# Scores ahead of value products in every beat of a cross attention, and another end of that stage

## The reference, cut to what matters

```python
q = (layernorm(x) @ wq.T + bq)            # 16 heads of 32
k = ctx @ wk.T + bk; v = ctx @ wv.T + bv  # 8 x 2048 x 512, the same width
attn = softmax(q @ k.T / sqrt(32), axis=-1)
x = x + (attn @ v) @ wo.T + bo            # y: the output projection
x = x + differential_attention(layernorm(x)); x = x + experts(layernorm(x))
```

## Time and profile before

| | us |
|---|---|
| median of 3 runs | 1677.9 |
| lowest, highest | 1677.11, 1684.54 |
| the profiled execution's own time | 1679.28 |
| its span, first to last instruction | 1677.5 |
| TensorE busy | 1608.8 (96%) |
| VectorE, ScalarE, GpSimd busy | 1166.9, 954.1, 932.3 |
| mean granted TensorE clock | 0.979 |

### The profile page before, as it was taken

How to read it: one execution, slowest core, us unless ns; L and a number is a source line. 1 busy time by engine, 2 the same in 40 slices (tenths; PEclk the granted TensorE clock), 3 DMA queues, 4 the chain that set the end, 5 groups by cost and what they waited for, 6 DMA issues and landing times. The chain is left out here.

```text
span 1677.5 us, 36990 instructions
## 1 busy us (share of the span) xinstructions
PE 1608.8 (96%) x15556; PEld 1302.3 (78%) x15556; DVE 1166.9 (70%) x1506; ACT 954.1 (57%) x1445; POOL 932.3 (56%) x498
## 2 busy tenths in 40 slices
PE   7999999999999999999999999677998899999999
PEld 6788888888888888888888888566886677777787
DVE  6137888888888888888888887756434677653322
ACT  4347677777677776777776776753102777630000
POOL 1227788788888878888887885322000344522220
PEclk9999999999999999999999999778999999899999
DMA  8422222222222222222222211203432111211001
GB/s 179 96 40 39 35 42 36 36 38 40 39 38 38 36 36 41 40 36 38 38 39 37 42 23 61 74 3 108 163 88 88 58 45 52 66 51 50 29 22 51
DMA packets 333876, 88.61 MB, mean 53 GB/s; under 512 B 284656, under 2 KB 317168, under 8 KB 333712
## 3 DMA queue, kind: packets, MB, share of 16 engines
q1 hardware_dynamic: 333712, 86.26, 23.0%
HBM read 71.60 MB, written 14.61 MB: 51 GB/s over the span
## 5 line engine op out<-in xcount | busy, mean ns | idle before, releaser
L766 POOL TENSOR_TENSOR b_acc<-b_acc,b_s 128x1024 f32<-128x1024 f32 x168 | 562.8, 3350 | 12.4 <-ACT b_s L1012 5.5
L1050 DVE TENSOR_TENSOR b_s<-b_s,b_mb 128x2048 f32<-128x2048 f32 x128 | 395.9, 3094 | 32.5 <-ACT b_mb L980 32.5
L1086 DVE TENSOR_TENSOR b_mx<-b_psS,b_mx 128x512 f32<-128x512 f32 x480 | 330.8, 689 | 103.0 <-PE b_psS L852 90.0
L1012 ACT ACTIVATE b_s<-b_s 128x2048 f32<-128x2048 f32 x128 | 244.3, 1909 | 13.8 <-DVE b_s L1050 10.6
L1029 ACT ACTIVATE b_s<-b_psS 128x2048 f32<-128x2048 f32 x128 | 241.1, 1884 | 15.9 <-DVE b_mx L1086 15.9
L43 PE MATMUL b_work<-wvT,cT 128*128 128x512 f32 x496 | 203.2, 410 | 0.0
L43 PE MATMUL b_work<-cT,wkT 128*128 128x512 f32 x496 | 200.2, 404 | 1.7 <-POOL b_ones L732 1.7
L44 PE MATMUL b_work<-cT,wkT 128*128 128x512 f32 x496 | 194.3, 392 | 0.0
L44 PE MATMUL b_work<-wvT,cT 128*128 128x512 f32 x496 | 194.2, 392 | 0.0
L45 PE MATMUL b_work<-wvT,cT 128*128 128x512 f32 x496 | 193.4, 390 | 0.0
L45 PE MATMUL b_work<-cT,wkT 128*128 128x512 f32 x496 | 193.2, 389 | 0.0
(11 more groups left out here) (315 smaller groups left out, 2815.8 us busy)
## 6 DMA issues: line engine op xcount, KB each, us to landing
cin<-in_ctx SPq DMA_DIRECT2D x496, 64.0 KB, 2.4
experts_sb<-in_L_ffn_expert_w SPq DMA_DIRECT2D x8, 1024.0 KB, 5.4
q_scratch<-d_st SPq DMA_DIRECT2D x16, 256.0 KB, 2.3
k_scratch<-d_st SPq DMA_DIRECT2D x16, 256.0 KB, 2.3
e_q<-q_scratch SPq DMA_DIRECT2D x16, 256.0 KB, 2.7
k_sb<-k_scratch SPq DMA_DIRECT2D x16, 256.0 KB, 2.9
b_kT<-in_x SPq DMA_DIRECT2D x4, 512.0 KB, 7.5
q_scratch<-a_q SPq DMA_DIRECT2D x8, 256.0 KB, 2.3
```

The costliest lines, as they stand in the source:

```text
L766: nc.gpsimd.tensor_tensor(acc[:, :, :], acc[:, :, :], s[:, buf, 2 * i:2 * i + 2, :], ALU.add).then_inc(sum_done, 1)
L1012: nc.scalar.activation(part, part, ACT.Exp, scale=SCALE).then_inc(exp_done, 1)
L1050: nc.vector.tensor_tensor(s[:, n % BUFS, :, :], s[:, n % BUFS, :, :], mb[:, :].rearrange("p (o n) -> p o n", o=1).broadcast_to([P, CHUNK, ...
L1086: nc.vector.tensor_tensor(mx[:, :, :], part, mx[:, :, :], ALU.max).then_inc(mx_done, 1)
```

## The change

In TensorE's queue `column_scores` comes first in a beat, ahead of `outputs` and of `denominators`. VectorE's and ScalarE's order in the slots stays. Behind `LATE`: the weights are turned in beats 257 and 259 and the tiles projected from beat 264 on; ScalarE does its late units after exponential and move instead of ahead of them; six tiles (`TILES`) are projected in this stage instead of seven, two of them added on VectorE (`add_tile`) straight from PSUM, four on GpSimd (`add`); GpSimd's late work has another order; the last chunk goes in two halves (`parts`), with its denominators ahead of its values (`last_outputs`); lambda's loads and first steps, four tiles' statistics and a first root come in this stage. `output_projection` projects tiles 6 and 7. A new class `Lambda` holds lambda's tiles and semaphores.

```diff
-        W_BEAT = {0: LATE + 5, 1: LATE + 5, 2: LATE + 7, 3: LATE + 7}
-        O_BEAT = {0: LATE + 8, 1: LATE + 9, 2: LATE + 12, 3: LATE + 13, 4: LATE + 15, 5: LATE + 17, 6: LATE + 20}
-        Y_BEAT = {0: LATE + 12, 1: LATE + 16, 2: LATE + 19, 3: LATE + 20, 4: LATE + 21, 5: LATE + 23, 6: LATE + 25}
-        TILES = B - 1
+        W_BEAT = {0: LATE + 1, 1: LATE + 1, 2: LATE + 3, 3: LATE + 3}
+        O_BEAT = {0: LATE + 5, 1: LATE + 7, 2: LATE + 9, 3: LATE + 11, 4: LATE + 13, 5: LATE + 17, 6: LATE + 21}
+        Y_BEAT = {0: LATE + 8, 1: LATE + 12, 2: LATE + 16, 3: LATE + 18, 4: LATE + 20, 5: LATE + 23}
+        TILES, ADDED = B - 2, 4
+        def parts(n):
+            if n < SLOTS * CHUNK - 1:
+                return [slice(0, CHUNK)]
+            return [slice(0, CHUNK // 2), slice(CHUNK // 2, CHUNK)]
...
+                        sp.dma_start(o_sb[:, g, 0:B - 1, :], o_d[g, 0:B - 1].rearrange("b p t -> p b t")
                                      ).then_inc(shared.o_in[0], 16)
+                    for i, name in enumerate(("lq1", "lq2", "lk1", "lk2")):
+                        sp.dma_start(consts.lam_in_sb[:, i, :], w_next[name]).then_inc(consts.lam_in, 16)
...
+            def add(t):
+                pool.wait_ge(shared.y_moved, t + 1)
+                nc.gpsimd.tensor_tensor(x1[:, t, :].rearrange("p (g d) -> p g d", g=G), o_sb[:, :, t, :],
+                                        x1[:, t, :].rearrange("p (g d) -> p g d", g=G), ALU.add).then_inc(shared.y_done, 1)
...
-                    for t in {LATE: (0, 1), LATE + 2: (2, 3), LATE + 4: (4, 5), LATE + 6: (6, 7)}.get(beat, ()):
-                        bias(t)
-                    for k in {LATE + 8: (0, 1), LATE + 10: (2, 3)}.get(beat, ()):
-                        weight_lo(k)
-                    for t in {LATE + 12: (0, 1), LATE + 14: (2, 3), LATE + 16: (4,), LATE + 18: (5,)}.get(beat, ()):
-                        output_lo(t)
-                if beat == LATE + 20:
+                    for work_of, n in {
+                            0: ((bias, 0), (bias, 1), (bias, 2)), 2: ((weight_lo, 0), (weight_lo, 1), (bias, 3)),
+                            4: ((weight_lo, 2), (weight_lo, 3)), 6: ((output_lo, 0), (bias, 4), (bias, 5)),
+                            8: ((bias, 6), (bias, 7), (output_lo, 1)), 10: ((output_lo, 2),),
+                            12: ((output_lo, 3), (add, 0)), 14: ((output_lo, 4),),
+                            16: ((add, 1),), 18: ((output_lo, 5),)}[beat - LATE]:
+                        work_of(n)
+                if beat == LATE + 22:
                     output_lo(6)
-            pool.wait_ge(sub_done, SLOTS * CHUNK)
-            for t in range(4):
-                add_tile(nc, pool, shared, t)
+            pool.wait_ge(sub_done, SLOTS * CHUNK + 1)
+            for t in range(2, ADDED):
...
                     pe.wait_ge(od_free, m)
...
+                    last = tile_outputs(n, i)
...
+                    if n == TAIL * CHUNK:
...
+                    for i in range(CHUNK):
+                        last = tile_denominators(n, i)
                 last.then_inc(pv_done, 1)
...
+            def last_outputs(n):
+                for i in range(0, CHUNK, 2):
+                    pe.wait_ge(exp_done, n + 1 + i // 2)
+                    for t in range(i, i + 2):
+                        last = tile_denominators(n, t)
+                    if i + 2 == CHUNK:
+                        last.then_inc(last_sums, 1)
+                    for t in range(i, i + 2):
+                        last = tile_outputs(n, t)
+                last.then_inc(pv_done, 1)
+            def tile_outputs(n, i):
+                m, c = divmod(n, CHUNK)
+                b, g = divmod(m, G)
+                at = value_places(b, c * CHUNK + i)[g]
+                for j in range(HG):
+                    last = nc.tensor.matmul(psO[j * HD:(j + 1) * HD, 0:P],
+                                            v[:, at + j * HD:at + (j + 1) * HD],
+                                            s[:, n % BUFS, i, j * P:(j + 1) * P],
+                                            start=c == 0 and i == 0, stop=c == CHUNK - 1 and i == CHUNK - 1)
+                return last
...
             for beat in range(FIRST, LAST):
+                if (n := score_step(beat)) is not None:
+                    column_scores(n)
                 for n in value_steps(beat):
-                    outputs(n)
+                    if n < SLOTS * CHUNK - 1:
+                        outputs(n)
+                    else:
+                        last_outputs(n)
                 if (m := sum_slot(beat)) is not None and m < TAIL:
                     denominators(m)
-                if (n := score_step(beat)) is not None:
-                    column_scores(n)
...
+                if (n := exp_step(beat)) is not None:
+                    for i, tiles in enumerate(parts(n)):
+                        act.wait_ge(sub_done, n + 1 + i)
+                        part = s[:, n % BUFS, tiles, :].rearrange("p t n -> p (t n)")
+                        nc.scalar.activation(part, part, ACT.Exp, scale=SCALE).then_inc(exp_done, 1)
...
+                if (n := move_step(beat)) is not None:
...
                 for k in late_units(W_BEAT, beat - 1):
                     i, bank = RING["W", k, 0], work[BANK["W", k, 0]]
                     act.wait_ge(work_full, i + 1)
                     nc.scalar.activation(wo_raw[:, k, :], bank[:, :], ACT.Copy)
                     nc.scalar.activation(woT[0][:, k, :], bank[:, :], ACT.Copy).then_inc(shared.wo_hi, 1)
-                for t in late_units(Y_BEAT, beat - 1):
+                for t in [t for t in late_units(Y_BEAT, beat - 1) if t < ADDED]:
                     i, bank = RING["Y", t, 0], work[BANK["Y", t, 0]]
                     act.wait_ge(work_full, i + 1)
                     nc.scalar.activation(o_sb[:, :, t, :], bank[:, :].rearrange("p (g d) -> p g d", g=G),
...
-                        act.wait_ge(shared.bo_done, B)
+                        act.wait_ge(split_done, SLOTS * CHUNK)
...
+            act.wait_ge(consts.lam_step, 2)
+            nc.scalar.activation(consts.lam_e[:, :], consts.lam_s[:, :], ACT.Exp).then_inc(consts.lam_exp, 1)
+            nc.scalar.activation(norm.root[:, :], ident[:, 0:B], ACT.Sqrt)
...
+            def reduce_maximum(m):
+                i, bank = RING["M", m, 0], work[BANK["M", m, 0]]
+                dve.wait_ge(work_full, i + 1)
+                reached(dve, spread_done, m - 1)
+                nc.vector.tensor_reduce(top[:, m % 2, :], bank[:, :].rearrange("p (j k) -> p j k", j=HG),
+                                        AX.X, ALU.max).then_inc(top_done, 1)
+            def add_tile(t):
+                dve.wait_ge(work_full, RING["Y", t, 0] + 1)
+                dve.wait_ge(shared.bo_done, t + 1)
+                nc.vector.tensor_tensor(x1[:, t, :], work[BANK["Y", t, 0]][:, :], x1[:, t, :], ALU.add).then_inc(y_added, 1)
...
             for beat in range(FIRST, LAST):
+                if (m := spread_slot(beat)) == SLOTS - 1:
+                    reduce_maximum(m)
...
+                    for tiles in parts(n):
+                        nc.vector.tensor_tensor(
+                            s[:, n % BUFS, tiles, :], s[:, n % BUFS, tiles, :],
+                            mb[:, :].rearrange("p (o n) -> p o n", o=1)
+                            .broadcast_to([P, tiles.stop - tiles.start, HG * P]),
+                            ALU.subtract).then_inc(sub_done, 1)
+                if (m := spread_slot(beat)) is not None and m < SLOTS - 1:
+                    reduce_maximum(m)
                 if (m := normal_slot(beat)) is not None:
                     if m == SLOTS - 1:
+                        for t in range(ADDED, TILES):
+                            add_tile(t)
+                        dve.wait_ge(consts.lam_in, 16 * 4)
+                        nc.vector.tensor_tensor(consts.lam_p[:, :, :], consts.lam_in_sb[:, 0:2, :],
+                                                consts.lam_in_sb[:, 2:4, :], ALU.mult).then_inc(consts.lam_step, 1)
                         for t in range(2):
+                            dve.wait_ge(shared.y_done, t + 1)
+                            norm.tile_stats(x1, t)
+                        dve.wait_ge(consts.lam_step, 1)
+                        nc.vector.tensor_reduce(consts.lam_s[:, :], consts.lam_p[:, :, :], AX.X,
+                                                ALU.add).then_inc(consts.lam_step, 1)
+                        for t in range(2, ADDED):
                             dve.wait_ge(shared.y_done, t + 1)
                             norm.tile_stats(x1, t)
                     if m < TAIL:
                         dve.wait_ge(od_full, m + 1)
+                    elif m < SLOTS - 1:
+                        dve.wait_ge(pv_done, (m + 1) * CHUNK)
                     else:
-                        dve.wait_ge(pv_done, (m + 1) * CHUNK)
+                        dve.wait_ge(last_sums, 1)
```

(83 more changed lines are left out.)

86 lines of the change are left out of this document (41 added, 45 removed).

## The result

The changed kernel took 1703.8 us (median of 4 runs, 1702.83 to 1704.52) against 1680.95 for the kernel before (4 runs, 1677.11 to 1684.54): a ratio of 1.0132 (95% interval 1.0107 to 1.0157), 22.9 us slower. The forecast was 1696.7 us, slower: the side is right and the time lies inside the range of 1684 to 1711, but 7 us above the forecast. Four of them are the difference itself, 22.9 where 18.8 was forecast; the other three are the starting point, as the forecast was added to a median of 1677.9 and the kernel before has 1680.95 with its fourth run. The profiled execution took 1703.61 us, with a span of 1701.8 us and a mean granted clock of 0.980.

A forecast was written before the change was run, and what follows sets the result against it. TensorE's queue was taken to bound the slots, and the loop of scores, maximum and move the tail. 32.1 - 6.8 - 5.5 - 1.0 = +18.8 us gave 1696.7 us, range 1684 to 1711 for 8 in 10.

The forecast's parts named there:

- slots: Cross attention slots: TensorE idles 1.19 us in beat 2 of 27 slots, +32.1 us (bounds +27 to +39).
- to the last scores: Tail from last projection to chunk 127's scores: 69.4 us before, 62.6 after, so -6.8 us (bounds -12, -2).
- to the end of the stage: Last scores to the end of cross attention: 35.0 us before, 29.5 after, so -5.5 us (bounds -10, 0).
- block: Block behind cross attention: steps removed, added tile work and a root on the path, -1.0 us (bounds -2.7, +1.5).
- the chain: Slots, reciprocal to maximum to move: next scores possible 7.43 us after the denominators start, 8.53 after beat 0's scores.
- two thin margins: Slots, beats 6 and 0: the move ends 0.08 and 0.10 us before TensorE needs it, so no wait.
- values with denominators: Stage's end, TensorE behind the last scores: value products and denominators take 3.6 us.
- subtractions: Stage's end, VectorE: four subtractions of 2.28 us each, ahead of slot 30's normalization.
- Adds, statistics and lambda's steps: Stage's end, VectorE: two added tiles of 0.67, four statistics of 0.63 and two lambda steps, 4.4 us.
- The faster one: Rival for the slots: no wait in beat 2, the tail's gains stand alone, 1664.6 us; chance 0.08.
- The one of 0.5 us: Rival for the slots: wait about 0.5 us as VectorE's operations are shorter, 13.5 us, time 1678.1; chance 0.06.
- The clock's fall: Rival for the slots: each wait drops TensorE's clock, 0.92 us more a slot, 1721.5 us, or 1773; chance 0.05.

The follow-up runs named there:

- e4: Changed kernel with VectorE's reciprocal and product behind the same beat's maximum, and ScalarE's bias on b_oq behind its move one beat later: 1666.0 us, ratio 0.9912.
- e6: Changed kernel with scores ahead of values only in beats behind the last projection, TensorE's old order in the slots: 1669.82 us, ratio 0.9923.
- the repair: Same run as e4: changed kernel with VectorE's maximum ahead of reciprocal and product, TensorE's order kept: 1666.0 us.
- the late-only kernel: Same run as e6: changed kernel with scores first only behind LATE: 1669.82 us; profiled again without an edit, 1666.4 us.
- e5: Changed kernel with VectorE's transpose of the context behind the same beat's maximum instead of ahead of it: 1683.92 us, ratio 1.0024.

## Why the prediction was right, and where it was 7 us short

| step | predicted | measured |
|---|---|---|
| slots | +32.1 | +31.3 |
| to the last scores | -6.8 | -7.4 |
| to the end of the stage | -5.5 | -3.3 |
| block | -1.0 | -2.6 |
| sum | +18.8 | +18.1 |
| code behind | 0 | +6.2 |
| span | +18.8 | +24.3 |

The sum of the four steps comes within 0.7 us, and in part by luck: the misses of 2.2 and 1.6 us have opposite signs.

**Slots: right in place and size.** Start by start the chain was as worked out (8.53, 7.43), the wait 1.12 instead of 1.19, once a slot. The two thin margins of 0.08 and 0.10 us held: the 26 waits of the window are one a slot. Taking the reciprocal out of the way (e4) or restoring the old order (e6) removes the whole of it.

**To the last scores: right in size.** The sum was 62.6 and the stretch took 61.98, in a second profile 62.94. What was not seen is how much the place of the cut decides: with the old order the new end takes 3.1 us more than the kernel before up to the last scores and 8.3 less behind them.

**To the end of the stage: 2.2 us too much gain.** The largest mis-sized term is values with denominators, 3.6 us at full clock. They ran from 1141.40 to 1146.70, 5.3 us, their first two groups at 1.83 and 1.95 us each against 1.08 and 1.06 at the full clock:

```profile
1141.00:1145.00 4.00, 4.00 (x91) 3.87 (x88) 2.77 (x4) 1.96 (x2) 1.30 (x1) 0.57 0.01 4
```

The clock of 0.57 is nearly its lower level (1.2 of 2.4 GHz), after TensorE had idled 2.03 us ahead of the scores. With it the turned maxima were reduced 9.9 us after the scores instead of 8.0. I had this as a bound, not in the value. The run with the denominators first has the same code here, and in its profile the clock stayed up (a granted clock of 1.00 from 1113 to 1117 us):

```profile
1112.26 1.17 PE L867 MATMUL b_psS<-b_q,b_kT 32*128 32x128 f32 x32 [2.04 <-ACT b_s L1048]
1113.36 1.08 PE L904 MATMUL b_psO<-b_s,v_sb 128*32 128x128 f32 x32
```

There the stretch takes 30.04 us, in the repair, with the clock up too, 30.09: the clock is 1.7 of the 2.2 us. The idle time ahead was 2.04 us, so the idle time by itself does not decide whether the clock falls. The rest lies in the subtractions, counted at 2.28 us each. Two of them took 5.59 together beside a split on GpSimd:

```profile
1155.62 5.59 DVE L1110 TENSOR_TENSOR b_s<-b_s,b_mb 128x2048 f32<-128x2048 f32 x2 [2.54 <-ACT b_mb L1017]
```

Adds, statistics and lambda's steps came about 0.4 us shorter than counted.

**Block: 1.6 us more gain.** VectorE's last splits took 0.56 and 0.29 us; in the kernel before, with GpSimd adding tiles beside them, the same lines took this:

```profile
1152.97 0.91 DVE L1229 TENSOR_TENSOR c_oT<-o_sb,c_oT 128x384 fp32r<-128x384 f32 x1 [1.56 <-ACT c_oT L1209]
1153.81 1.35 DVE L1232 TENSOR_TENSOR c_oT<-b_o,c_oT 128x128 fp32r<-128x128 f32 x1
```

That is 2.26 - 0.85 = 1.4 us, which the sum left out. That GpSimd is the reason is argued from the two timelines, no run varied it alone. The Trainium skill ("SBUF — State Buffer", section "SBUF: two separate sides") has the two engines share one port pair that only one of them holds at a time; the rows agree in direction.

**Code behind: the step that the prediction did not have.** It took the untouched 501.4 us over. The changed kernel showed 507.7 in both its profiles; the late-only kernel showed 507.7 once and 500.5 once. So 6.2 of the 24.3 us by which the spans differ lie in code that the edit did not touch. The medians hold less of it. The changed kernel's four runs lie within 1.7 us of each other, and both its profiles have the long code behind. The kernel before has two runs at 1677.11 and 1677.9 and two at 1684.0 and 1684.54, and its median of 1680.95 lies between. Its two profiles (1679.28 and 1678.84 us) have 501.4 and 501.5 us behind; the kernel with only the denominators' place changed, profiled at 1684.19 us, has 506.3. So the upper pair probably has a long code behind as well. Then 22.9 us hold about 3 of the 6.2, and against the upper pair (median 1684.3) the change costs 19.5 us, where 18.8 was forecast. This is argued, as no profile caught the kernel before at 1684. The table has lengths between the two as well (502.9 to 504.4). Whether the edit makes the long one likelier, and what makes the clock fall, stays open.

**The rivals.** The faster one needed a chain shorter by 1.19 us: e5 shortens it, by half, and e4 takes it off the path to the maximum. The one of 0.5 us needed shorter operations on VectorE; they kept their lengths (0.96, 0.29, 0.70, 2.83). The clock's fall is refuted for the slots: 26 waits of 1.1 us between 200 and 1060 us, with a granted clock of 1.00 in that stretch. The section "A second HAM failure mode: psum-queue depth-cycling" of the Trainium skill ("TensorE: Matmul & The Clock Gate") would have let it fall; this trace does not bear that out for waits of this size.

## What to carry to other kernels

When an instruction is moved in one engine's queue, follow its consumers through the queues of the others: if those still take the results in the old order, the move makes them wait for the later one and hands the wait round the loop. An engine that is busy all the time (here 100.00 of 100 us) can't be helped by order, only hurt: keep the new order where the engine has idle time (here behind `LATE`), or move the consumers with it. Before costing an edit against one profile, take a second profile of unchanged code: here one kernel's untouched part took 500.5 us in one and 507.7 in the other, more than most terms under study. And cut the time at more than one place: a gain up to the last scores can be work that was moved behind them.

## What was not expected of the hardware

The same kernel, twice: granted clock 0.88 and 0.95 in the same 100 us, and 507.7 against 500.5 us for the same code. After an idle time of 2.03 us ahead of the same scores TensorE's clock fell in the changed kernel; after 2.04 us it stayed up in the run with the denominators first. A split of 128x128 on VectorE took 0.29 us, and 1.35 us where GpSimd was adding tiles.
